# State recurrence by pairs of tiles: one product and one scan of 2048 columns, with unrolled rounds and six PSUM banks in the feed-forward stages

## What is computed

```python
x = x + 0.5 * ffn(layernorm(x))
x = x + mixer(layernorm(x))
x = x + 0.5 * ffn(layernorm(x))

def ffn(x):                       # fp4(a): blocks of 16, scale max/6, rounded to a 4-bit grid
    h = silu(fp4(x) @ fp4(w_gate).T) * (fp4(x) @ fp4(w_up).T)        # 704 wide
    return fp4(h) @ fp4(w_down).T

def mixer(h):
    x, z = split(norm(h) @ in_proj_w)                # 512 each
    x = silu(causal_conv4(x))
    dt, Bm, Cm = split(x @ x_proj_w)                 # 64, 16, 16
    delta = softplus(dt @ dt_proj_w + dt_proj_b)
    for each channel d (512), state n (16), along the 1024 tokens t:
        h[t] = exp(delta[t] * A[d, n]) * h[t-1] + delta[t] * x[t] * Bm[t, n]
    y[t, d] = sum over n of h[t, d, n] * Cm[t, n] + x[t, d] * D[d]
    return (y * silu(z)) @ out_proj_w
```

## Time and profile before

| | us |
|---|---|
| median of 3 runs (lowest, highest) | 3286.45 (3285.9, 3291.64) |
| the profiled execution's own time | 3285.56 |
| its span, first to last instruction | 3283.5 |
| PE busy | 2736.3 |
| DVE busy | 2652.0 |
| POOL busy | 2174.0 |
| ACT busy | 1695.5 |

### The profile page before, as it was taken

One profiled execution on the slowest core, in us unless ns is written; L12 is line 12 of the kernel. 1 busy time (PEld: TensorE's weight loads), 2 busy tenths in 40 slices (PEclk: granted clock), 3 DMA queues, 4 the chain that ended last, 5 costly groups with the idle time before them and its releaser, 6 DMA issues. The chain is left out here.

```text
span 3283.5 us, 33864 instructions
## 1 busy us (share of the span) xinstructions
PE 2736.3 (83%) x10349; PEld 1403.1 (43%) x10349; DVE 2652.0 (81%) x2498; ACT 1695.5 (52%) x2363; POOL 2174.0 (66%) x1219
## 2 busy tenths in 40 slices
PE   3999999776878978868878868978867659999998
PEld 1565656453324424414414414424412125555565
DVE  6777777408999999989999989999999946777774
ACT  3444444335756656656665655666654513444442
POOL 4566665306887877767778777777787735555552
PEclk9999999887978979969978968979966679999999
DMA  3011111108687676776777766776767720111000
GB/s 102 20 49 42 46 48 39 51 11 204 145 192 177 165 190 171 172 186 158 175 186 175 181 163 171 180 180 167 183 170 184 187 78 13 33 33 32 26 26 20
DMA packets 173331, 388.08 MB, mean 118 GB/s; under 512 B 22502, under 2 KB 90150, under 8 KB 172902
## 3 DMA queue, kind: packets, MB, share of 16 engines
q1 hardware_dynamic: 155382, 367.06, 45.0%
q10 hardware_dynamic: 17776, 18.94, 1.9%
HBM read 308.26 MB, written 52.49 MB: 110 GB/s over the span
## 5 line engine op out<-in xcount | busy, mean ns | idle before, releaser
L962 POOL TENSOR_TENSOR mix_scan<-mix_scan,mix_bc 128x1024 f32<-128x1024 f32 x512 | 1204.5, 2355 | 423.0 <-DVE mix_scan L1117 422.7
L1117 DVE TENSOR_TENSOR_SCAN mix_scan<-mix_decay,mix_ps_du 128x1024 f32<-128x1024 f32 x512 | 1170.0, 2285 | 72.8 <-ACT mix_decay L1063 23.5
L1129 DVE TENSOR_TENSOR mix_ps_du<-mix_ps_du,mix_bc 128x1024 f32<-128x1024 f32 x512 | 618.5, 1208 | 148.2 <-PE mix_ps_du L1230 142.3
L1230 PE MATMUL mix_ps_du<-mix_stack,mix_sel 96*128 96x512 bf16 x1024 | 367.9, 447 | 394.2 <-DVE mix_scan L1117 360.9
L711 PE MATMUL ffn_ps_gate_up<-ffn_w_gate_up,ffn_xT 128*128 128x512 f32 (+1 forms) x1536 | 662.3, 568 | 14.6 <-DVE ffn_h L479 13.0
L1063 ACT ACTIVATE mix_decay<-mix_decay,mix_a_neg 128x1024 f32<-128x1024 f32 x512 | 573.5, 1141 | 116.1 <-DMA mix_decay<-delta_rows 115.2
L741 PE MATMUL ffn_ps_down<-ffn_w_down,ffn_hT 128*128 128x256 f32 (+1 forms) x1536 | 386.4, 394 | 12.4 <-ACT ffn_hT L638 12.4
L711 PEld LDWEIGHTS ffn_ps_gate_up<-ffn_w_gate_up,ffn_xT 128*128 128x128 f32 x1536 | 273.4, 191 | 281.4 <-issue 231.2
L1230 PEld LDWEIGHTS mix_ps_du<-mix_stack,mix_sel 96*128 96x128 bf16 x1024 | 78.9, 103 | 707.3 <-DVE mix_scan L1117 581.6
L1212 PE MATMUL mix_ps_y<-mix_scan,mix_red 128*32 128x512 f32 x2048 | 342.1, 750 | 5.4 <-POOL mix_scan L962 5.4
L479 DVE TENSOR_TENSOR ffn_h<-ffn_silu_gate,ffn_ps_gate_up 128x704 f32<-128x704 f32 x128 | 113.6, 887 | 279.1 <-ACT ffn_silu_gate L643 279.1
(11 more groups left out here) (133 smaller groups left out, 3638.5 us busy)
## 6 DMA issues: line engine op xcount, KB each, us to landing
mix_decay<-delta_rows SPq DMA_DIRECT2D x512, 512.0 KB, 6.8
mix_stack<-mix_parts SPq DMA_DIRECT2D x384, 64.0 KB, 2.0
delta_rows<-mix_delta SPq DMA_DIRECT2D x32, 512.0 KB, 3.1
ffn_x<-_attn_hidden_states_dram SPq DMA_DIRECT2D x32, 256.0 KB, 2.9
after_ffn<-ffn_y SPq DMA_DIRECT2D x32, 256.0 KB, 3.0
normed_ffn<-ffn_y_normed SPq DMA_DIRECT2D x32, 256.0 KB, 3.0
mix_x_tokens<-normed_ffn SPq DMA_DIRECT2D x32, 256.0 KB, 11.8
mix_x_residual<-after_ffn ACTq DMA_DIRECT2D x32, 256.0 KB, 2.9
```

The source lines that it names most:

```text
L962: G.tensor_tensor(wt, wt, bc[:, r % 2, 1, :], ALU.mult).then_inc(hc_done, 1)
L1117: V.tensor_tensor_scan(w[:, slot % RING, :], da[:, slot % SPREADS, :], ps_du[:, slot % 2, :], 0.0, ALU.mult, ALU.add).then_inc(scan_done, 1)
L1129: V.tensor_tensor(ps_du[:, slot % 2, :], ps_du[:, slot % 2, :], bc[:, r % 2, 0, :], ALU.mult)\
L1230: ins = M(ps_du[:, slot % 2, h * 512:(h + 1) * 512], const.sel[0:SEL, i, :], stack[:, c % 2, q, h * 512:(h + 1) * 512], start=True, stop=True)
```

## The change

In the mixer DVE takes two slots at once: one product over both halves of `ps_du`, written to two places of the ring `w`, and one scan of 2048 columns over them in place. So that the state starts from zero in the second tile, the decay's first column of every odd place is zero: it is set once, and the spread and the exponential of odd slots leave that column out. The C product takes two slots too. Replication fills both halves of `ps_du` for the next pair once the product has read them. The wait for the reduction (`y_made`), which guards the reuse of `w`, moves from the scan to the product. The spreads wait by pairs. The sums over the states are placed by pairs: one half behind the jobs, one behind the replication. The rounds are written out without a loop.

In the FFN the turned x and `down` get no banks of their own beyond one: `down` has 256 columns in one bank for both t, the first half of the turned x the other 256 columns there, and the second half the last 256 columns of the second bank of the turned h. The turning and the copying of x are done in two halves, and new waits keep the sharers of a bank apart.

The diff, cut:

```diff
-    psH = ps_turned[:, :, :].rearrange("p a b -> p (a b)")
-    psX = a.ps("x_turned", [P, 512])
-    psD = a.ps("down", [P, 2, 512])
+    psT = ps_turned[:, :, :].rearrange("p a b -> p (a b)")
+    psDX = a.ps("down", [P, 2, D])
+    psH, psD = psT[:, 0:KH * P], psDX[:, 0, :]
+    psX = [psDX[:, 1, :], psT[:, KH * P:KH * P + D]]
...
-            V.scalar_tensor_tensor(y[:, (j - 2) % 4, t, :], psD[:, t, 0:D], 0.5, x[:, (j - 2) % 8, t, :],
+            V.scalar_tensor_tensor(y[:, (j - 2) % 4, t, :], psD, 0.5, x[:, (j - 2) % 8, t, :],
                                    ALU.mult, ALU.add).then_inc(sig.y_done, 1)
...
             A.activation(hT[0:LASTK, t, (KH - 1) * P:KH * P],
                          psH[0:LASTK, (KH - 1) * P:KH * P], ACT.Copy).then_inc(sig.hT_kept, 1)
 
+        def keep_x(t, j, i):
+            act.wait_ge(sig.x_turned, i * 2 + (t + 3))
+            if t == 0 and on(j, i, -1):
+                act.wait_ge(sig.gate_up_done, i * 2)
+            A.activation(xT[:, (j + 1) % 2, t * D:(t + 1) * D], psX[t], ACT.Copy).then_inc(sig.xT_kept, 1)
...
+            if on(j, i, 1):
+                keep_x(0, j, i)
             if on(j, i, -2):
                 keep_h(1, j, i)
             if on(j, i, 0):
                 silu(1, j, i)
             if on(j, i, 1):
-                act.wait_ge(sig.x_turned, i + 2)
-                if on(j, i, -1):
-                    act.wait_ge(sig.gate_up_done, i * 2)
-                A.activation(xT[:, (j + 1) % 2, :], psX[:, :], ACT.Copy).then_inc(sig.xT_kept, 1)
...
-                if t == 0:
-                    pe.wait_ge(sig.xT_kept, i + 1)
+                pe.wait_ge(sig.xT_kept, i * 2 + (t + 1))
...
+            if t == 0 and on(j, i, 0):
+                pe.wait_ge(sig.xT_kept, i * 2 + 2)
...
+        def turn_x(t, j, i):
+            if t == 0:
+                pe.wait_ge(sig.xq_done, i + 2)
+                if on(j, i, -2):
+                    pe.wait_ge(sig.y_done, i * 2 - 3)
+            elif on(j, i, -2):
+                pe.wait_ge(sig.hT_kept, i * 2 - 2)
+            for k in range(KX):
+                n = t * KX + k
+                ins = nc.tensor.transpose(psX[t][:, k * P:(k + 1) * P], xq[:, (j + 1) % 2, n * P:(n + 1) * P],
+                                          ident[:, :])
             ins.then_inc(sig.x_turned, 1)
...
+            if on(j, i, -3) or (t == 1 and on(j, i, -2)):
+                pe.wait_ge(sig.y_done, i * 2 + (t - 4))
+            if t == 1 and on(j, i, 1):
+                pe.wait_ge(sig.xT_kept, i * 2 + 3)
             for k in range(KH):
                 c = min(P, F - k * P)
-                ins = M(psD[:, t, 0:D], hT[0:c, t, k * P:(k + 1) * P], wd[0:c, k, :],
+                ins = M(psD, hT[0:c, t, k * P:(k + 1) * P], wd[0:c, k, :],
...
                     gate_up(t, j, i, 0)
+                if t == 1 and on(j, i, 1):
+                    turn_x(0, j, i)
                 if on(j, i, -2):
                     turn_h(t, j, i)
                 if on(j, i, 0):
                     gate_up(t, j, i, 1)
-                if t == 1 and on(j, i, 1):
-                    turn_x(j, i)
                 if on(j, i, -2):
                     down(t, j, i)
+                if t == 1 and on(j, i, 1):
+                    turn_x(1, j, i)
...
 
-            pairs = (B - 2) // 2
-            for r in range(-1, 1):
-                program(r, r, False)
-            if pairs > 0:
-                with eng.Fori(0, pairs) as it:
-                    for k in range(2):
-                        program(1 + k, it * 2 + (1 + k), True)
-            for r in range(1 + 2 * pairs, B + 1):
+            for r in range(-1, B + 1):
                 program(r, r, False)
...
-                n = R * 64 + (slot + 1)
                 if s == 0:
                     sy.wait_ge(delta_kept, 16 * chunk(R, c))
-                elif slot >= SPREADS or r > 0:
-                    sy.wait_ge(scan_done, n - SPREADS + (1 if s == SLOTS - 1 else 0))
+                if slot >= SPREADS or r > 0:
+                    sy.wait_ge(scan_done, R * 32 + (slot - SPREADS) // 2 + 1)
                 row = c * P + 32 * (s % 4) + 8 * (s // 4)
-                sy.dma_start(da[:, slot % SPREADS, :],
-                             delta_dram[r % 2, row:row + NCH, :].unsqueeze(0).to_broadcast([NST, NCH, L]))\
+                lo = slot % 2
+                sy.dma_start(da[:, slot % SPREADS, lo:],
+                             delta_dram[r % 2, row:row + NCH, lo:].unsqueeze(0).to_broadcast([NST, NCH, L - lo]))\
                   .then_inc(spread_in[slot % SPREADS], 16)
...
+                    if slot % 2 == 0 and core(r, full):
+                        pool.wait_ge(scan_done, R * 32 + (slot // 2 + 1))
+                        wt = w[:, slot % RING:slot % RING + 2, :]
+                        G.tensor_tensor(wt, wt, both(bc[:, r % 2, 1, :]), ALU.mult).then_inc(hc_done, 1)
...
+            for k in range(1, SPREADS, 2):
+                ins = G.memset(da[:, k, 0:1], 0.0)
+            ins.then_inc(reset_set, 1)
...
+                        decay = da[:, at % SPREADS, at % 2:]
+                        A.activation(decay, decay, ACT.Exp, scale=const.aneg[:, qi:qi + 1]).then_inc(exp_done, 1)
...
+            def pair(ring, p):
+                k = 2 * p % ring.shape[1]
+                return ring[:, k:k + 2, :]
+
+            def product(r, R, p):
+                dve.wait_ge(rep_du, R * 32 + (p + 1))
+                if p == 0:
+                    dve.wait_ge(taken["B"], (R + 1) * 4)
+                if p >= RING // 2 or r > 0:
+                    dve.wait_ge(y_made, R * 16 + (2 * p + 1 - RING) // 4 + 1)
+                V.tensor_tensor(pair(w, p), ps_du[:, :, :], both(bc[:, r % 2, 0, :]), ALU.mult).then_inc(dbu_done, 1)
+
+            def scan(r, R, p):
+
+                dve.wait_ge(exp_done, R * 64 + (2 * p + 2))
+                dve.wait_ge(dbu_done, R * 32 + (p + 1))
+                state = pair(w, p).rearrange("p a l -> p (a l)")
+                V.tensor_tensor_scan(state, pair(da, p).rearrange("p a l -> p (a l)"), state, 0.0,
                                      ALU.mult, ALU.add).then_inc(scan_done, 1)
 
             def program(r, R, full):
-                nxt = full or r + 1 < B
...
-                        n = R * 64 + (slot + 1)
-                        dve.wait_ge(rep_du, n)
-                        if slot == 0:
-                            dve.wait_ge(taken["B"], (R + 1) * 4)
-                        V.tensor_tensor(ps_du[:, slot % 2, :], ps_du[:, slot % 2, :], bc[:, r % 2, 0, :], ALU.mult)\
-                         .then_inc(dbu_done, 1)
-
+                        product(r, R, slot // 2)
...
-                    pe.wait_ge(hc_done, R * 64 + 4 * (m + 1))
+                    pe.wait_ge(hc_done, R * 32 + 2 * (m + 1))
...
+                if p > 0 or r > 0:
+                    pe.wait_ge(dbu_done, R * 32 + p)
+                for k in range(2):
+                    i, q = divmod(s + k, 4)
+                    for h in range(2):
+                        ins = M(ps_du[:, k, h * 512:(h + 1) * 512], const.sel[0:SEL, i, :],
+                                stack[:, c % 2, q, h * 512:(h + 1) * 512], start=True, stop=True)
                 ins.then_inc(rep_du, 1)
...
+                for p in range(32):
+                    rr, R2, at = ahead(r, R, 2 * p, 2)
+                    if core(rr, full):
+                        replicate(rr, R2, at // 2)
+                    m, odd = divmod(p - 2, 2)
+                    if odd and (core(r, full) if m >= 0 else (full or r >= 1)):
+                        sum_quad(*((r, R, m) if m >= 0 else (r - 1, R - 1, 15)), 1)
                     for sl, kind, rel, n, bank, prev in jobs:
-                        if sl == slot:
+                        if sl // 2 == p:
                             if prev is not None:
                                 pk, prel, pn = prev
                                 pe.wait_ge(taken[pk], nth(pk, R + prel, pn))
                             make(r, R, kind, rel, n, bank)
+                    if not odd and (core(r, full) if m >= 0 else (full or r >= 1)):
+                        sum_quad(*((r, R, m) if m >= 0 else (r - 1, R - 1, 15)), 0)
```

More of the change, by code:

```diff
@@ L886, in core, with both @@
             return full or 0 <= r < B
+        def both(row):
+            return row.unsqueeze(1).to_broadcast([P, 2, L])
         def ahead(r, R, slot, by):
@@ L1139, in program @@
                     if core(r, full):
-                        scan(r, R, slot)
+                        scan(r, R, slot // 2)
+            dve.wait_ge(reset_set, 1)
             rounds(dve, program)
@@ L1219, in sum_quad, with replicate @@
                     ins.then_inc(y_made, 1)
[L1221 to L1224 removed]
+            def replicate(r, R, p):
+                c, s = divmod(2 * p, SLOTS)
                 if s == 0:
                     pe.wait_ge(stacked[c % 2], 16 * 12 * (R * 2 + (c // 2 + 1)))
[L1227 to L1231 removed]
+                if p > 0 or r > 0:
```

(17 more changed lines are left out.)

36 lines of the change are left out of this document (4 added, 32 removed).

## The result

The changed kernel takes 3914.32 us (median of 4 runs, 3911.33 to 3917.99) against 3287.19 us before: ratio 1.1905, 95% interval 1.1885 to 1.1926. The prediction was 3986 us, with 3830 to 4200.

The account below looks back on a forecast made before the run. The prediction took DVE to bound the mixer and PE the FFN stages. From 3285.6 us it added 696 us for turns between scan and POOL in the mixer and 4 us in the FFN: 3986 us, range 3830 to 4200.

Parts of the forecast that it names:

- Turns: Mixer: the scan with both operands in SBUF and POOL's instructions exclude each other; +696 us, chance 0.80.
- DVE's own work: Mixer: double products and scans save fixed parts, 130 and 152 ns a pair, together 72 us less.
- POOL's C product over a pair: Mixer: two single C products less one fixed part, 4.52 us, at most 4.71.
- full turns: Mixer: each engine waits out the other's whole instruction; 154 us of possible overlap kept for the range.
- chunk operations: Mixer: four further POOL operations in each chunk of 16 slots also take turns, 9.0 us a chunk.
- second cost: Mixer: scan waiting for replication, two slots' jobs and exponential; forecast took replication as nothing, late jobs 0 (0 to 60).
- The rest of the mixer: Mixer outside the turns: replication nothing, late jobs 0 (0 to 60 us), transfers 0 (0 to 30).
- The straight code: Mixer rounds written out: fewer loop ends against more code to load, 0 us (-10 to +20).
- The FFN stages: FFN, bound by PE: new waits there count in full, +4 us, bounds 0 and 22.
- stall foreseen for the second "down": FFN: the second "down" loses cover for the copy of h; at most 0.1 us, 64 x 0.07 = +4 us.
- Rival B: Mixer: the scan doesn't lock POOL out and the pair form pays, 3218 us, down to 3180; chance 0.12.
- Rival C: Mixer: POOL can't start during a scan but doesn't hold it up, 3570 us; chance 0.07.

Follow-up runs that it names:

- run 2: The changed kernel with POOL's C product on 768 of the 1024 columns of each tile, the rest left out: 3681.0 us.
- run 3: The kernel before, single tiles, with DVE's product written to the scan ring in SBUF and the scan reading it there: 3878.9 us.
- run 1: The changed kernel with POOL's C product cut to the first column of each tile: 3445.9 us.
- run 9: The changed kernel with the exponential 4 slots ahead and POOL's C product replaced by four memsets a pair: 3407.9 us.
- run 4: The changed kernel with the product kept in PSUM, the scan reading it there and the replication waiting for the scan: 4725.4 us.
- run 5: The changed kernel with the exponential 4 slots ahead instead of 2, nothing left out: 3885.98 us, ratio to the kernel before 1.1828.
- lead 2: The exponential 2 slots ahead, as in both kernels; with it the changed kernel with the cut C product takes 3445.9 us.
- run 10: The kernel before with the change's straight code alone, the mixer's rounds written out instead of looped: 3254.22 us against 3284.53, ratio 0.9913.
- run 11: The kernel before with the change's FFN part alone: 3280.22 us, ratio 0.9989.
- lead 4: The exponential 4 slots ahead instead of 2; here on the changed kernel with the C product cut to one column of each tile: 3368.1 us.

## Why the prediction was right, point by point

**Turns**, the mechanism that carried the forecast, is shown: runs 2 and 3 have it in size, run 3 from one edit. Run 1 takes the C product away, run 9 puts writes in its place, and run 4 puts the scan's operand back into PSUM; in each the exclusion goes. The Trainium skill (SBUF — State Buffer, Who interferes with whom) says that a GpSimd instruction that only writes SBUF doesn't contend with a DVE instruction of two SBUF inputs; run 9 agrees, with memsets of 834 to 856 ns under scans of 4.42 us. The other half of the rule as the prediction has it, that the first holds the ports for its whole instruction, the page writes of DVE's two-port modes, and of the shared ports in general it says that they are an exclusive lock. Here it holds nearly: a scan ends 0.14 us sooner behind the C product than full turns would have it.

**DVE's own work.** Product 2286 ns forecast, 2261 measured; scan 4418, shortest 4424. The fixed part of about 154 ns is real and saved: two single products take 155 ns more than the double one, two scans 146.

**POOL's C product over a pair:** 4.52 forecast, median 4522 ns.

**The size** was 696 + 4 against 633 us. The step that was off is full turns, for which the text kept 154 us in the range. A plain pair was put at 4.42 + 4.52 + 2 x 0.07 = 9.08 us and takes 8.87: the scan ends 0.14 us sooner after POOL's end than its own 4.42, and of the two hand-overs only the one from scan to C product (0.08 us) is left. That is 0.21 x 256 = 54 us. The chunk operations were put at 9.0 us a chunk and add 2 x 2.05 + 2 x 1.8 = 7.7: 1.3 x 31 = 40 us. Against these 94 us stands the second cost that I set at zero, 28 us by run 5: 696 - 94 + 28 = 630, the loop's measured growth. Run 5 bears this out: its loop takes 2508 us, and 2602 - 94 is 2508. The two errors, 94 and 28 us, have opposite signs, so the total owes a little to luck.

**The rest of the mixer at nothing.** The replication was judged with its own 1.8 us. What is queued behind it on PE (the jobs of two slots), then on ACT (the exponential), wasn't followed to the scan. Under turns it costs 28 us. Without the C product the pair form is 159 us slower than the kernel before at lead 2 (run 1: 3446 against 3287), though DVE's own work is 72 us less.

**The straight code** was put at 0, from -10 to +20, and no row showed these bounds. In the kernel before it gives 30 us back (run 10), outside them. What it is worth in the changed kernel isn't tested; the sum above closes without it. The odd tiles' transfers, put at 0 too, land in 6.8 us as before.

**The FFN stages:** +4 forecast, -4 measured (run 11), which is hardly more than can be told from no change. The stall foreseen for the second "down" doesn't show: between 60 and 640 us PE waits 6.7 us for the copy of h before and 6.5 in run 11. Where the 4 us come from isn't shown.

**Rival B** (no turns, 3218 us) was very likely wrong also in its price: with C products out of the way the pair form takes 3446 us, or 3368 with lead 4, and less the 49 us that the chunk operations' turns cost at most, 3319. **Rival C** (one-way blocking, 3570) is out by run 2.

**Signs in the profile.** Loop near 2600 us (2536), product 2.29 (2.26), scans 6 to 7 us (6.44), clock under 0.85 (0.77), FFN as before: right. "POOL hardly idle" was wrong: it is idle 670 us before C products, since in a plain pair it waits for the scan by semaphore, with nothing else queued, and that wait is the scan's turn.

## What to carry to other kernels

Before an operand of a long DVE instruction moves from PSUM to SBUF, add up POOL's reading instructions beside it: from then on both sums lie on one path, whatever is saved in fixed costs. When work is grouped in pairs, follow what is queued behind each wait to the engine that needs it; here the jobs of two slots stood there where it had been one. And try the by-products of a change alone: here the straight code was worth 0.9% while the change it came with cost 19%.

## What the runs showed of the hardware that was not expected

POOL's memsets run unhindered under a scan that blocks its products (run 9), and its products run unhindered under the same scan once one of the scan's operands lies in PSUM (run 4). The hand-over is not a clean cut: a scan ends 4.28 us after POOL's end where it takes 4.42 alone, and a blocked chunk operation 2.15 us after the scan's where it takes 2.36. The ends of POOL's records are rough, but the distance of two products is not: 8.86 us less the C product's 4.50 leaves 4.36 for scan and hand-over. With POOL already blocked at the hand-over a single-tile slot takes 4.30 us, with POOL waiting by semaphore 4.58 (run 3). And the loop, three passes of two rounds of some 238 us each, cost 30 us (run 10).
